# Attention value sums of a graph and mixture-of-experts layer: one f32 product per item, or many products over f16 halves

## The reference

```python
x = x + gnn(layernorm(x))                  # 1250 rows of 512, 20000 edges
# the second half: 4 experts, top 2 of 4 for each row
for e in range(4):
    h = ln(xf, ln1_w, ln1_b)
    q, k, v = split(h @ ipw.T + ipb, 3)    # 8 heads of 64
    scores = einsum('htd,hsd->hts', q, k) / sqrt(64)
    scores = where(mask[None, None, :], scores, NEG)      # keys: rows of this expert and slot
    a = softmax(scores, axis=-1)
    o = einsum('hts,hsd->htd', a, v).transpose(1, 0, 2).reshape(T, E)
    o = o @ opw.T + opb
    x1 = xf + o
    m = gelu(ln(x1, ln2_w, ln2_b) @ w1.T + b1) @ w2.T + b2
    out += where(mask[:, None], (x1 + m) * w, 0)
```

## Time and profile before

| | |
|---|---|
| median of 3 runs | 1281.78 us (1280.66 to 1286.93) |
| profiled execution, first to last instruction | 1278.3 us |
| PE busy in it | 1050.9 us (82%), 5155 matmuls |
| VectorE busy | 734.6 us (57%) |
| ScalarE busy | 455.7 us (36%) |
| GpSimd busy | 320.2 us (25%) |
| mean granted TensorE clock | 0.920 of full speed |
| chain that ended last | PE 64%, VectorE 15%, issue 11%, ScalarE 5% |

### The profile page before, as it was taken

How to read it: one execution, slowest core, us unless ns; L and a number is a source line. 1 busy time by engine, 2 the same in 40 slices (tenths; PEclk the granted TensorE clock), 3 DMA queues, 4 the chain that set the end, 5 groups by cost and what they waited for, 6 DMA issues and landing times.

```text
span 1278.3 us, 19543 instructions
## 1 busy us (share of the span) xinstructions
PE 1050.9 (82%) x5155; PEld 566.6 (44%) x5156; DVE 734.6 (57%) x1609; ACT 455.7 (36%) x850; POOL 320.2 (25%) x300
## 2 busy tenths in 40 slices
PE   3897877899955878688776989899797999889974
PEld 2554655678622433334343434344343335433333
DVE  4587425142285587536874574856748248646753
ACT  2201211122333554436625334434344532336521
POOL 3103322334348535114511030000000133313211
PEclk9998979899966989899897989999999999989997
DMA  5590000000246515101413020000002121110010
GB/s 153 143 270 1 2 3 4 3 0 1 97 164 193 141 48 195 53 28 49 169 36 124 1 66 1 1 0 0 0 0 100 34 61 50 76 39 1 2 32 35
DMA packets 34846, 75.90 MB, mean 59 GB/s; under 512 B 8203, under 2 KB 8501, under 8 KB 34474
## 3 DMA queue, kind: packets, MB, share of 16 engines
q1 hardware_dynamic: 26122, 55.91, 14.0%
q0 software_dynamic: 8320, 16.49, 4.4%
q10 hardware_dynamic: 288, 2.10, 0.5%
HBM read 49.06 MB, written 26.70 MB: 59 GB/s over the span
## 4 chain that ended last, share of the span: by engine, by line
PE 64%; DVE 15%; issue 11%; ACT 5%; DMA 1%; DVEq 1%; POOL 1%; SPq 1%; ACTq 0%; POOLq 0%
PE bank L1444 16%; PE bank L1535 9%; PE bank L1288 8%; PE bank L1328 5%; PE bank L1565 4%; PE bank L1620 3%; DVE den L2303 3%; PE bank L1499 2%; PE bank L1322 2%; PE bank L1520 2%; PE bank L1522 2%; PE bank L1249 2%; DVE oT L2305 1%; PE bank L1579 1%; PE bank L1441 1%
## 5 line engine op out<-in xcount | busy, mean ns | idle before, releaser
L1914 DVE TENSOR_SCALAR oh_src<-iota,edge 125x1250 f16 x178 | 102.3, 575 | 121.4 <-PE bank L1288 114.8
L1535 PE MATMUL bank<-probs_t,v_head 128*128 128x512 f32 (+1 forms) x288 | 147.0, 594 | 7.0 <-ACT probs_t L1058 6.4
L1058 ACT ACTIVATE probs_t<-bank 128x512 f32<-128x512 f32 x144 | 81.5, 573 | 135.9 <-PE bank L1522 135.4
L2216 DVE TENSOR_REDUCE mx<-bank 128x1 f32<-128x512 f32 x144 | 88.5, 656 | 64.0 <-PE bank L1499 63.0
L1288 PE MATMUL bank<-oh_src,oh_dst 125*125 x534 | 114.7, 366 | 3.7 <-DVE oh_dst L1916 0.9
L590 POOL TENSOR_TENSOR w<-w_stage,w 128x1024 f16<-128x1024 f32 x35 | 75.8, 2176 | 132.9 <-ACT w L860 132.9
L1620 PE MATMUL bank<-probs_t,v_head 128*128 128x128 f32 (+2 forms) x192 | 88.1, 546 | 6.9 <-ACT probs_t L1109 5.1
L1288 PEld LDWEIGHTS bank<-oh_src,oh_dst 125*125 x534 | 72.3, 146 | 46.5 <-issue 27.8
L1444 PE MATMUL bank<-hT,w 128*128 128x256 f16 (+1 forms) x552 | 89.2, 325 | 1.5 <-DVE hT L2148 1.5
L1565 PE MATMUL bank<-hT,w 128*128 128x512 f16 x288 | 72.8, 386 | 7.8 <-ACT t L1083 7.8
L1444 PE MATMUL bank<-w,hT 128*128 128x512 f16 x264 | 68.5, 415 | 8.8 <-DVE hT L2148 8.8
(11 more groups left out here) (323 smaller groups left out, 1913.0 us busy)
## 6 DMA issues: line engine op xcount, KB each, us to landing
w_stage<-in_ew_dram SPq DMA_DIRECT2D x40, 512.0 KB, 4.3
lists<-zeros SPq DMA_DIRECT2D x1, 10340.0 KB
x_in<-lists SPq DMA_DIRECT2D x15, 517.0 KB, 6.2
x_mem<-lists SPq DMA_DIRECT2D x3, 1024.0 KB, 5.2
x_mem<-lists SPq DMA_DIRECT2D x1, 2560.0 KB, 10.1
out_dram<-x_mem SPq DMA_DIRECT2D x10, 250.0 KB
table<-rows SPq DMA_DIRECT2D x5, 449.8 KB
big<-in_x_dram SPq DMA_DIRECT2D x10, 224.0 KB
```

The lines of the kernel that those rows point to most:

```text
L1058: nc.scalar.activation(probs_t[:, x % NPB, 0:cn], stb[x % 2][:, 0:cn], ACT.Exp).then_inc(s_exp, 1)
L1535: nc.tensor.matmul(pvb[(hd * nq + s) % 2][:, 0:cn], v_head[:, hd, kt, :], probs_t[:, (hd * nx + i) % NPB, 0:cn], start=(k == 0), stop=(k = ...
L1914: nc.vector.tensor_scalar(oh_src[:, bass.ds(slot, 1), i, 0:N].rearrange("p a n -> p (a n)"), iota[:, :], edge[:, 0, i, bass.ds(g, 1)], Non ...
L2216: nc.vector.tensor_reduce(mx[:, hd, t, s:s + 1], sbk[i % 2][:, 0:cn], AX.X, ALU.max).then_inc(s_mx, 1)
```

## The change

The value sum of an item is made of f16 operands, and the roles of the two operands are exchanged. The stationary operand is now 128 query columns of the probabilities, and the moving operand is the head's 64 values with one column of ones, 65 columns (`HC`). The probabilities are two halves: ACT takes the exponential of the same bank twice, once into `p_hi` in f16 and once into `p_all` in f32 (two buffers, `NP32`), and the low half `p_lo = p_all - p_hi` is a subtraction on VectorE in the long body and on GpSimd in the short ones. The values are two halves as well, `v_hi` (with the ones) and `v_lo`. An item of 512 columns thus has 12 products: 4 high by high (65 columns), 4 high by low values (64), and 4 low by high (65). The first eight (`high_sums`) follow the item's exponential; the last four (`low_sums`) come one item later. The turned scores of an item wait until the second exponential of the item two before has been taken (`s_all` in place of `s_exp`). The row of maxima has a constant added so that the f16 half stays in range.

The result now has queries in the partitions, so its denominator is one column a tile: VectorE takes a reciprocal of up to 4 columns and multiplies (`normalise_heads`, into `o_rows`), PE turns the pair's 128 columns back (`turn_heads`), ACT adds the bias into the high half (`high_heads`) and VectorE makes the low half (`low_heads`). In the long body head 1 of a pair and head 0 of the next now run as one sequence of 36 items; the loop begins with the projection. GpSimd no longer copies values; VectorE makes the low halves of the next expert's first weights (`low_piece`), beside the last heads, all six casts of them on ACT in the last head. The numbers of unread products are smaller. The next expert's rows are loaded after the attention, where they were loaded within it.

```diff
--- before.py
+++ after.py
...
+NP32 = 2
+HC = HD + 1
+RAISE = 32.0
...
-WARM_SHORT, WARM_LONG, WARM_ROUTE = 18, 32, 31
+WARM_SHORT, WARM_LONG, WARM_ROUTE, WARM_TURN = 12, 12, 31, 5
...
-        v_head = sb("v_head", [P, 2, NTL, P], F32)
+        v_hi = sb("v_hi", [P, NTL, H * HC], F16)
...
-        probs_t = sb("probs_t", [P, NPB, 512], F32)
-        normal = probs_t
...
+        p_hi = sb("p_hi", [P, NPB, 512], F16)
+        p_lo = sb("p_lo", [P, NPB, 512], F16)
...
+                    for u in range(H):
+                        for i in range(nx):
+                            low_probs(u * nx + i, 0)
+                        if u < NWP - QKV_P:
+                            low_weights(e, QKV_P + u)
+                        if u in (0, 2, 4):
+                            pool.wait_ge(s_lo, raw.at((u + 1) * nx))
+                            pool.wait_ge(s_elo, e * NWP + QKV_P + min(u, NWP - QKV_P - 1) + 1)
+                            second_head(u // 2 + 1)
...
+                def exponential(x, x0):
+
+                    s, c0, cn, kt, k, nk = shape.items[x % nx]
+                    b = x0 + x
+                    act.wait_ge(s_sT, scored.at(x + 1))
+
+                    act.wait_ge(s_pv, summed.at(x - 3))
+                    nc.scalar.activation(p_hi[:, b % NPB, 0:cn], stb[b % 2][:, 0:cn], ACT.Exp).then_inc(s_exp, 1)
+
+                    act.wait_ge(s_lo, lows.at(x - 1))
+                    nc.scalar.activation(p_all[:, b % NP32, 0:cn], stb[b % 2][:, 0:cn], ACT.Exp).then_inc(s_all, 1)
...
+                    act.wait_ge(s_scat, 16 * 2 * NT)
                     for u in range(H):
                         short_head(u)
...
+                def weighted(bank, probs, kt, cols, n, first):
+
+                    for t in range(n):
+                        last = nc.tensor.matmul(bank[:, t * HC:(t + 1) * HC], probs[:, t * P:(t + 1) * P],
+                                                v_hi[:, kt, cols], start=first and t == 0, stop=True,
+                                                skip_group_check=True)
+                    return last
...
-                    pe.wait_ge(s_exp, made)
-                    nc.tensor.matmul(pvb[(hd * nq + s) % 2][:, 0:cn], v_head[:, hd, kt, :],
-                                     probs_t[:, (hd * nx + i) % NPB, 0:cn], start=(k == 0),
-                                     stop=(k == nk - 1)).then_inc(s_pv, 1)
...
+                    pe.wait_ge(s_exp, exped.at(g + 1))
+                    weighted(bank, probs, kt, value_cols(j, hd), cn // P, k == 0)
+                    for t in range(cn // P):
+                        nc.tensor.matmul(bank[:, t * HC:t * HC + HD], probs[:, t * P:(t + 1) * P],
+                                         v_lo[:, kt, low_cols(j, hd)], start=False, stop=True, skip_group_check=True)
+
+                def low_sums(j, hd, i, g, b):
+
+                    s, c0, cn, kt, k, nk = shape.items[i]
+                    pe.wait_ge(s_lo, lows.at(g + 1))
+                    weighted(pvb[(hd * nq + s) % 2], p_lo[:, b % NPB, 0:cn], kt, value_cols(j, hd), cn // P,
+                             False).then_inc(s_pv, 1)
...
+                    for g in range(n):
+                        (j, hd, beside), i = heads[g // nx], g % nx
+                        high_sums(j, hd, i, g, x0 + g, g // nx * nq + shape.items[i][0])
+                        if g > 0:
+                            before, h = heads[(g - 1) // nx][0:2]
+                            low_sums(before, h, (g - 1) % nx, g - 1, x0 + g - 1)
+                        if g + 2 < n:
+                            scores_t(heads[(g + 2) // nx][1], (g + 2) % nx, g + 2)
                         if beside is not None:
                             for k in scores_beside(nx, i):
                                 scores(beside, k)
...
-                        attend(j, 0, 1)
-                        project(j + 1, ns)
+                        project(j + 1, ns, lambda: last_sums(j, 0, nx - 1))
                         maxima_row(1)
-                        attend(j, 1, 0)
+                        attend([(j, 1, 0), (j + 1, 0, 1)], nx)
...
+                    step(nc.vector.reciprocal(r_den[:, 0:n].unsqueeze(2), sums[:, :, HD:HC]))
+                    nc.vector.tensor_tensor(o_rows[:, t0:t0 + n, hd * HD:(hd + 1) * HD], sums[:, :, 0:HD],
+                                            r_den[:, 0:n].unsqueeze(2).broadcast_to([P, n, HD]),
+                                            ALU.mult).then_inc(s_on, 1)
...
-                    step(nc.vector.reciprocal(den[:, cols], den[:, cols]))
-                    step(nc.vector.tensor_tensor(o_pair[:, cols], o_pair[:, cols], den[:, cols], ALU.mult))
-                    step(nc.vector.tensor_scalar(o_hi, mine, ep_pair[:, 2:3], None, ALU.add))
-                    nc.vector.scalar_tensor_tensor(o_lo, mine, ep_pair[:, 2:3], o_hi, ALU.add,
-                                                   ALU.subtract).then_inc(s_oT, 1)
...
+                    dve.wait_ge(s_othi, high_o.at(made))
+                    nc.vector.scalar_tensor_tensor(oT[1][:, pair, cols], bank[:, 0:n].unsqueeze(1), bias,
+                                                   oT[0][:, pair, cols], ALU.add, ALU.subtract).then_inc(s_oT, 1)
...
+                def low_probs(x, x0):
+
+                    s, c0, cn, kt, k, nk = shape.items[x % nx]
+                    b = x0 + x
+                    dve.wait_ge(s_all, raw.at(x + 1))
+                    nc.vector.tensor_tensor(p_lo[:, b % NPB, 0:cn], p_all[:, b % NP32, 0:cn], p_hi[:, b % NPB, 0:cn],
+                                            ALU.subtract).then_inc(s_lo, 1)
...
+                        if g == nx:
+                            scored_t.skip(nx)
+                            second_head_copies()
                         if beside is not None:
...
+                            for k in scores_beside(nx, g % nx):
+                                maximum(beside, k)
+                        for s, at in turns:
+                            if at + 2 == g:
+                                low_of(s)
+                        for p, h, s, at in norms:
+                            if at == g:
+                                normalise_heads(h, s, p * nx + ends_of(s))
+                        low_probs(g, x0)
...
```

586 lines of the change are left out of this document (329 added, 257 removed).

## The result

| | before | changed |
|---|---|---|
| median | 1282.08 us | 1417.26 us (1410.17 to 1418.67) |
| ratio | | 1.108, 95% interval 1.102 to 1.114 |
| span of the profiled execution | 1278.3 us | 1415.3 us |
| mean granted TensorE clock | 0.920 | 0.811 |

The median before is of four runs here. Every ratio in this document compares only the fast runs of both kernels, those within 1.5% of the fastest of their kernel, while the times are medians of all runs; so a time of 1276 us can stand beside a ratio of 1.008 where the median before was 1281.

A forecast was written before the change was run, and what follows sets the result against it. PE was taken as the bound, without slack in the long body; the change would put a closed PE-VectorE wait there. 1278.3 + 72 (long body) - 4 (short bodies) = 1346 profiled, 1350 us median, range 1305 to 1405.

The forecast's parts named there:

- The ring: Long-body items with wide scores: PE and VectorE wait for each other, 3.11 us an item against 1.73, +77 over 56 items.
- the rival: Long body: PE works about half the time, clock falls to 1.2 GHz, +0.9 us an item, 1407 us; chance 0.14.
- The long body without the clock: Long attention at full clock: all its terms together were forecast at +72 us.
- turns of a pair: Long body: waits of 1.52 and 3.34 us and about 1.3 of half clock go, three times; net -14 us.
- end: End of the long attention: 9.4 us before the first output product become about 4, -5 us.
- normalisations: Long body: one per head on VectorE inside the closed wait, taken as 0.7 us each, +5 us.
- The small product: Value sum: each of the 12 products taken at 0.058 us, from rows with 125-column loads and 8-column products.
- The short bodies: The three short attentions, with +3 for the first expert's start, were forecast at -4 us together.
- GpSimd's turn: Short bodies: low halves queue behind GpSimd's weights and copies, so PE waits about 3 us in heads 1 and 3.
- the wide reciprocals: Each of two 384-column short bodies: waits of 3.76 and 2.53 us and some 3.7 of half clock go, -10 us.
- GpSimd's terms: Short bodies: PE's waits for GpSimd's low halves, +6.5 us in each 384-column body and +8 in the third.
- The start: First expert: exponentials now wait for the scattered rows, +3 us.

The follow-up runs named there:

- The two edits of order: Each on the changed kernel, long body: VectorE's low half moved ahead of the maxima, 1295.22 us; or PE's low products moved behind the plain scores, 1297.62 us.
- the filled ring: Changed kernel plus eight unread PE products in each long-body item with scores beside it, ahead of the wait for the low half; 1383.06 us, 1.078.
- the weights off GpSimd: Kernel with the long body's low halves on GpSimd (1276 us), the short bodies' remaining weight low halves moved from GpSimd to VectorE; 1250.17 us, 0.976.
- both waits away: Kernel with the long body's low halves on GpSimd (1276 us), constant written early and ScalarE's wait for scattered rows moved later in the first expert; 1272.11 us, 0.996.
- the filled short heads: Kernel of the gaining edits together (1248.99 us) plus eight unread PE products at the start of each of heads 4 to 7 in the short bodies; 1247.01 us, 0.977.
- the kernel without the filling: Changed kernel with long-body low halves on GpSimd, short-body weight low halves on VectorE, and the first expert's two early waits removed; 1248.99 us, 0.975.

## Why the prediction was right or wrong

**The ring: right, and its length nearly.** The order of the two engines was read correctly. At full clock the ring took 2.93 us where 3.11 were forecast; the releasers are those named. The two edits of order show that it is the cause.

**The clock: the first of two steps that failed.** The sum left the clock at full speed, and the rival had 0.14, because I took PE for busy near 6 of 10 in the ring, like the stretch at full clock in the earlier trace rows. By my own prices it was less, 12 x 0.058 + 0.88 = 1.58 of 3.11 us, 0.51. Measured it was busy 1.41 of 2.93 us, 0.48, between the two stretches of the earlier trace rows, and the clock fell within two items. So these rows gave no ground for either side, and 0.14 was too sure. The rival's mechanism and nearly its price were on record (0.9 us a turn; measured 0.73). The clock cost 41 us, as the filled ring shows. That the rival's 1407 us came near the measured 1417 is luck all the same: it had 57 for the clock, 72 for the rest of the long body and a gain in the short ones.

**The long body without the clock: 72 forecast, 54 measured.** The pair iteration took 107.9 us; in the run with the filled ring it took 102.6, and without the 5.8 at the loop's beginning 96.8, where I had said near 96. That agreement is in part luck: the terms of the sum add up to 99 for a pair. Over the whole long attention 95.4 less 41 leaves 54, and the sum had 72. So with the clock in it the forecast for the long body would have been 113, 18 too long. The turn of the ring explains 10 of these (56 x 0.18), and the small products below more of them; turns of a pair, end and normalisations were not measured one by one.

**The small product: mis-sized by two.** The term was 0.058 us, from the earlier trace rows. It is 0.030: four take 0.12 to 0.13 us in the attention and 0.030 each by themselves. The row had loads of 125 columns and the change has 128. That hid what the change is worth: a value sum of 12 products takes 0.36 us instead of 0.86. At full clock an item without scores repeated every 0.98 us (837.70, 838.68, 839.66), bound by ScalarE's two exponentials, where I had 1.2; behind the ring, at half clock, it was 1.51.

**The short bodies: the second step that failed, -4 forecast, about +39 with the start.** GpSimd's turn was right (3 us in heads 1 and 3; 3.41 and 3.40 measured). What failed is the other side of the sum: the 10 us for the wide reciprocals, 2.5 and 3 for the rest. Without GpSimd's terms (6.5, 6.5 and 8) the sum had the three attentions 28 us shorter than before; with the weights off GpSimd they last 215.8 us, where they lasted 216.3 before. The waits behind the reciprocals are gone, but in these heads PE now waits in small pieces for ScalarE's rows (5.3 us in the first body) and VectorE's last heads (2.4), and its clock there is 0.71 instead of 0.90. That these small waits eat the expected gain is what the waits suggest; I made no run that takes them away, so this cause stays open.

**The start: +3 forecast, +11.9.** 2.9 of it is no effect of the change: the part ahead ended that much later in this execution, and the same instruction came anywhere from 370.9 to 376.3 us in ten of the profiled kernels. The scatter took 4.8. The 4.2 for the constant was not in the prediction at all; I had read the addition as free and not asked which engine writes the constant, nor where that stands in its queue. With both waits away the first value sum came at 427.9, and the wait moved to GpSimd's first low half.

**The sum of the misses.** The time was 67 us above the forecast: 41 for the clock, 43 for the short bodies with the start, 18 less for the rest of the long body, and 1 for what is left. Either of the first two alone would have stayed inside the range.

## What to carry to other kernels

Where a change splits one operation between two engines, write down for each what stands ahead of it on both; if each waits behind the other, add the pieces up to a ring, and then break it by moving one group past another: here 120 us for no instruction less. Such a ring can cost twice: here the granted clock fell from 1.00 to 0.50 within two items and lengthened TensorE's part of each turn, 41 us in all, so work out a regular wait at the lower clock too. Take the price of an operation from a row of the same shape, to the column, and if none has it, keep the far end as a case of its own; and don't count on a higher clock by itself: in the first short attention it rose from 0.74 to 0.86 and the length stayed (75.9 and 75.2 us).

## What the runs showed that was not expected

- A load of 128 f16 columns vanishes behind a product of 65 columns (0.030 us a product); one of 125 columns doesn't (0.059).
- TensorE's clock fell to 0.50 while PE was busy all the time, behind 48 products with loads of 128 and 8 moving columns and within 48 with loads of 125 and 8.
- With eight unread products an item in the loop of the long body PE stood for 4.3 us at the loop's beginning, where it had been 0.7. The trace names no cause.
- The part ahead of the experts, the same in all kernels but for the place of one constant, was once much shorter: the arms were computed at 369.0 to 376.3 us in 14 profiled executions, and at 356.8 in that of the filled short heads. There the granted clock was 1.00 between 200 and 250 us, where the kernel without the filling had 0.86, with this line:

```profile
200.00:250.00 50.00, 40.36 (x256) 29.88 (x254) 15.42 (x46) 8.25 (x20) 14.07 (x11) 0.86 0.01 3
```
